# Keys and values of the first attention: seven part products (Strassen, in Winograd's form) for four of the five row blocks

## The reference

```python
xn = layernorm(x)
x = x + gnn(xn, W, edge_weight, src, dst) + mix(xn)      # L0
# mix:
ln1 = layer_norm(xn, gamma1, beta1)
q, k, v = ln1 @ wq, ln1 @ wk, ln1 @ wv                    # (625, 1024) each, 16 heads of 64
qp, kp = relu(q) + 0.001, relu(k) + 0.001
kvs = einsum('lhm,lhd->hmd', kp, v); ksum = sum(kp, 0)
att = einsum('lhm,hmd->lhd', qp, kvs) / einsum('lhm,hm->lh', qp, ksum)
add1 = att @ wo + xn
```

## Time and profile before

| | us |
|---|---|
| median of 3 runs | 1765.59 |
| lowest, highest | 1764.76, 1766.38 |
| span of the profiled execution | 1762.0 |
| TensorE busy | 1715.6 (97%) |
| VectorE busy | 743.4 (42%) |
| ScalarE busy | 396.1 (22%) |
| GpSimd busy | 653.0 (37%) |

### The profile page before, as it was taken

One profiled execution on the slowest core, in us unless ns is written; L12 is line 12 of the kernel. 1 busy time (PEld: TensorE's weight loads), 2 busy tenths in 40 slices (PEclk: granted clock), 3 DMA queues, 4 the chain that ended last, 5 costly groups with the idle time before them and its releaser, 6 DMA issues. The chain is left out here.

```text
span 1762.0 us, 21030 instructions
## 1 busy us (share of the span) xinstructions
PE 1715.6 (97%) x8016; PEld 1068.0 (61%) x8016; DVE 743.4 (42%) x1549; ACT 396.1 (22%) x740; POOL 653.0 (37%) x537
## 2 busy tenths in 40 slices
PE   9999999998999999999999999898999999999998
PEld 6466445544444677755477775555776676677633
DVE  5886011322732432154455553854333322222237
ACT  1100000001411000111177771841100222222232
POOL 0666884031000047767787862000210312222213
PEclk9999999998999999999999999999999999999999
DMA  9654116074170034333322223705262899999951
GB/s 352 200 168 123 2 1 167 1 214 120 73 297 5 0 96 127 98 96 101 92 49 57 53 48 79 195 11 195 60 198 87 351 415 415 400 415 411 412 150 59
DMA packets 103755, 281.71 MB, mean 160 GB/s; under 512 B 61745, under 2 KB 69155, under 8 KB 91282
## 3 DMA queue, kind: packets, MB, share of 16 engines
q1 hardware_dynamic: 28755, 218.54, 33.4%
q0 software_dynamic: 67872, 50.79, 12.8%
q10 hardware_dynamic: 7052, 11.35, 1.9%
HBM read 250.37 MB, written 29.80 MB: 159 GB/s over the span
## 5 line engine op out<-in xcount | busy, mean ns | idle before, releaser
L608 POOL DMA_INDIRECT table_d<-wring x85 | 173.9, 2046 | 106.3 <-issue 66.7
L380 PE MATMUL bank<-wring,region_a 128*125 128x512 f32 x480 | 207.6, 593 | 1.7 <-DVE region_a L754 0.7
L993 POOL DMA_INDIRECT wring<-xl_d,wring x85 | 111.2, 1308 | 255.2 <-DMA xr_d<-flat_b 229.3
L380 PEld LDWEIGHTS bank<-wring,region_a 128*125 128x125 f32 x480 | 89.7, 188 | 115.3 <-issue 113.9
L1006 POOL DMA_INDIRECT score_d<-wring x85 | 108.8, 1280 | 72.1 <-DMA score_d<-wring 42.7
L396 PE MATMUL bank<-flat_d,wring 128*128 128x312 f32 (+1 forms) x512 | 135.0, 426 | 0.0
L2403 PEld LDWEIGHTS bank<-picked_t,wring 128*128 128x128 f32 x1152 | 129.4, 192 | 7.7 <-issue 7.7
L2403 PE MATMUL bank<-picked_t,wring 128*128 128x128 f32 x1152 | 131.3, 276 | 0.0
L993 POOL DMA_INDIRECT wring<-xr_d,wring x85 | 110.4, 1299 | 25.9 <-issue 24.7
L396 PEld LDWEIGHTS bank<-flat_d,wring 128*128 128x128 f32 x512 | 96.8, 189 | 37.8
L2410 PE MATMUL bank<-wring,small_t 128*64 128x256 f32 x640 | 76.0, 393 | 2.8 <-PEq L2037 2.8
(11 more groups left out here) (441 smaller groups left out, 2671.6 us busy)
## 6 DMA issues: line engine op xcount, KB each, us to landing
wring<-in_experts SPq DMA_DIRECT2D x57, 2048.0 KB, 19.5
wring<-in_L_Ws SPq DMA_DIRECT2D x6, 2048.0 KB, 15.8
table_d<-eq_buf SPq DMA_DIRECT2D x2, 3072.0 KB, 26.9
score_d<-no_edge SPq DMA_DIRECT2D x2, 3072.0 KB, 32.1
wring<-table_d POOLq DMA_DIRECT2D x10, 610.4 KB, 7.1
wring<-score_d SPq DMA_DIRECT2D x5, 1093.8 KB
wring<-pid_d ACTq DMA_DIRECT2D x17, 312.5 KB, 3.8
wring<-in_edge_w ACTq DMA_DIRECT2D x17, 312.5 KB, 4.4
```

Of the source, the lines that this page charges most:

```text
L380: ins = pe.matmul(bank[0:R, :], act_t[:, k, tok(t)], w[:, k * HALF:(k + 1) * HALF], start=(k == 0), stop=(k == chunks - 1))
L608: pool.indirect_dma_start(out=tables_d[b % 2], out_offset=bass.IndirectOffsetOnAxis(ap=edge_at[:, b:b + 1], axis=0), in_=edge_sums[:, b, : ...
L993: pool.indirect_dma_start(out=to[:, g % 2, j, :], out_offset=None, in_=table, in_offset=bass.IndirectOffsetOnAxis(ap=index[:, b:b + 1], ax ...
```

## The change

For the first four row blocks, keys and values are now made by `pe_gemm_seven` in TensorE, `dve_gemm_seven` in VectorE and `act_gemm_seven` in ScalarE. The inputs are taken as 2 x 2 parts: A11, A12, A21, A22 (two row blocks of 250 rows, four pieces of the inner dimension each) and B11, B21, B12, B22 (four inner pieces, 512 columns each). Seven part products are made where the ordinary way has eight; every one is two row blocks by four pieces. Their inputs are sums: S1 to S4 of the activations, which lie in `pair_sums` (the freed `eq_buf` and a part of `rows_b`), and T1 to T4 of the weights, made in place in the weights' slots. The names in FILLS are TensorE's tiles in order, STEPS are VectorE's, COPIES are ScalarE's; each list is one semaphore. p1 and p2 share a bank, so do p7 and p4, and p5 and p3: the second is added to the first, after it has been read. The fifth row block is multiplied as before, and ScalarE copies it. The clip of the keys is no longer part of the reading of a bank: VectorE does it when all keys are in SBUF, in five passes, and TensorE waits for these ahead of line 551. The two slots of a matrix are freed near its end, the left one after p5_1, the right one after p3_1. So that the new semaphores fit, four of the second layer are replaced by older ones, with offsets.

```diff
--- before.py
+++ after.py
@@ -136,6 +136,35 @@
         return self.ring[:, slot, :]
 
 
+class Seven:
+    FILLS = ("last_left", "p1_0", "p1_1", "last_right", "p2_0", "p2_1", "p7_0", "p7_1", "p6_0", "p6_1",
+             "p4_0", "p4_1", "p5_0", "p5_1", "p3_0", "p3_1")
+    STEPS = ("s3", "s1_early", "s2", "t3", "t2", "t4", "s1", "u2_0", "u3_0", "u2_1", "u3_1", "t1", "s4",
+             "c21_0", "c21_1", "c22_0", "c22_1", "c12_0", "c12_1")
+    COPIES = ("c_left", "p1_0", "p1_1", "c_right", "c11_0", "c11_1")
+    def __init__(self, n, filled, stepped, copied):
+        self.filled, self.stepped, self.copied = filled, stepped, copied
+        self.fill_from, self.step_from, self.copy_from = (n * len(x) for x in (self.FILLS, self.STEPS, self.COPIES))
+    def copy(self, name):
+        return self.copy_from + self.COPIES.index(name) + 1
+    def fill(self, name):
+        return self.fill_from + self.FILLS.index(name) + 1
+    def step(self, name):
+        return self.step_from + self.STEPS.index(name) + 1
 def tok(t):
     return slice(t * R, (t + 1) * R)
 
@@ -413,6 +442,115 @@
                     ins.then_inc(d_filled, 1)
             wt.free(dring.filled, dring.made)
 
+        seven_sems = sem("seven_filled"), sem("seven_stepped"), sem("seven_copied")
+        X, W, Y, Z = (4, 5), (0, 1), (6, 7), (2, 3)
+        def pe_gemm_seven(pe, x, f, sums, before=None):
+            left = wt.take(pe)
+            def tile(bank, at, weights, k0, done, start=True):
+                for k in range(4):
+                    ins = pe.matmul(banks[bank][0:R, :], at(k), weights[:, (k0 + k) * HALF:(k0 + k + 1) * HALF],
+                                    start=start and k == 0, stop=k == 3, skip_group_check=not start)
+                if done:
+                    ins.then_inc(f.filled, 1)
+            def rows(k0, t):
+                return lambda k: x[:, k0 + k, tok(t)]
+            def summed(n, p):
+                return lambda k: sums[n][:, k, tok(p)]
+            def until(name):
+                pe.wait_ge(f.stepped, f.step(name))
+            def last(bank, weights):
+                for k in range(K):
+                    ins = pe.matmul(banks[bank][0:R, :], x[:, k, tok(T - 1)], weights[:, k * HALF:(k + 1) * HALF],
+                                    start=(k == 0), stop=(k == K - 1))
+                ins.then_inc(f.filled, 1)
+            last(Y[1], left)
+            if before:
+                pe.wait_ge(before.copied, before.copy("c11_1"))
+            for p in range(2):
+                tile(X[p], rows(0, p), left, 0, True)
+            right = wt.take(pe)
+            last(Y[0], right)
+            for p in range(2):
+                pe.wait_ge(f.copied, f.copy(f"p1_{p}"))
+                tile(X[p], rows(4, p), left, 4, True, start=False)
+            until("t3")
+            if before:
+                pe.wait_ge(before.stepped, before.step("c12_1"))
+            else:
+                dring.wait_empty(pe)
+            for p in range(2):
+                tile(Z[p], summed(0, p), right, 0, True)
+            until("t2")
+            pe.wait_ge(f.copied, f.copy("c_right"))
+            for p in range(2):
+                tile(Y[p], summed(1, p), left, 0, True)
+            until("t4")
+            for p in range(2):
+                until(f"u3_{p}")
+                tile(Z[p], rows(4, 2 + p), left, 4, True, start=False)
+            until("t1")
+            for p in range(2):
+                tile(W[p], summed(0, p), left, 0, True)
+            wt.free(f.filled, f.fill("p5_1"))
+            until("s4")
+            for p in range(2):
+                until(f"c22_{p}")
+                tile(W[p], summed(1, p), right, 4, True, start=False)
+            wt.free(f.filled, f.fill("p3_1"))
+        def act_gemm_seven(s, f, place, shaped):
+            for name, fill, bank, t, h in (
+                    ("c_left", "last_left", Y[1], T - 1, 0), ("p1_0", "p1_0", X[0], 0, 1), ("p1_1", "p1_1", X[1], 1, 1),
+                    ("c_right", "last_right", Y[0], T - 1, 1), ("c11_0", "p2_0", X[0], 0, 0),
+                    ("c11_1", "p2_1", X[1], 1, 0)):
+                s.wait_ge(f.filled, f.fill(fill))
+                s.activation(place(t, h), shaped(banks[bank][0:R, :]), ACT.Copy).then_inc(f.copied, 1)
+        def dve_gemm_seven(v, x, f, sums, slots, place, shaped, finish=None):
+            a11, a12 = x[:, 0:4, 0:2 * R], x[:, 4:8, 0:2 * R]
+            a21, a22 = x[:, 0:4, 2 * R:4 * R], x[:, 4:8, 2 * R:4 * R]
+            b11, b21, b12, b22 = (wring[:, slot, k0 * HALF:(k0 + 4) * HALF] for slot in slots for k0 in (0, 4))
+            def step(name, out, in0, in1, op=ALU.add, fill=None, after_step=None):
+                if fill:
+                    v.wait_ge(f.filled, f.fill(fill))
+                if after_step:
+                    v.wait_ge(f.stepped, f.step(after_step))
+                v.tensor_tensor(out, in0, in1, op).then_inc(f.stepped, 1)
+            def bank(n):
+                return shaped(banks[n][0:R, :])
+            step("s3", sums[0], a11, a21, ALU.subtract)
+            step("s1_early", sums[1], a21, a22)
+            step("s2", sums[1], sums[1], a11, ALU.subtract, after_step="s1_early")
+            step("t3", b12, b22, b12, ALU.subtract, fill="last_right")
+            step("t2", b11, b12, b11, after_step="t3")
+            step("t4", b21, b21, b11, ALU.subtract, fill="p2_1", after_step="t2")
+            step("s1", sums[0], a21, a22, fill="p7_1")
+            for p in range(2):
+                v.wait_ge(f.copied, f.copy(f"p1_{p}"))
+                step(f"u2_{p}", place(p, 1), bank(Y[p]), place(p, 1), fill=f"p6_{p}")
+                step(f"u3_{p}", place(2 + p, 1), bank(Z[p]), place(p, 1), after_step=f"u2_{p}")
+            step("t1", b11, b22, b11, ALU.subtract, fill="p6_1", after_step="t4")
+            step("s4", sums[1], a12, sums[1], ALU.subtract, after_step="s2")
+            for p in range(2):
+                step(f"c21_{p}", place(2 + p, 0), bank(Z[p]), place(p, 1), fill=f"p4_{p}", after_step=f"u2_{p}")
+            for p in range(2):
+                step(f"c22_{p}", place(2 + p, 1), bank(W[p]), place(2 + p, 1), fill=f"p5_{p}", after_step=f"u3_{p}")
+            for p in range(2):
+                step(f"c12_{p}", place(p, 1), bank(W[p]), place(p, 1), fill=f"p3_{p}", after_step=f"u2_{p}")
         def rows_tiles(v, halves=2):
 
             for h in range(halves):
@@ -471,7 +609,11 @@
         seen = above(CH_B)
         sel = above(CH_B)
         assert upper_at[0] <= 2 * 4096
-        kvs = rows_b.rearrange("p s k c -> p (s k c)")[:, 0:K * 2 * (DH + 1)].rearrange("p (k d) -> p k d", k=K)
+        KVS = K * 2 * (DH + 1)
+        kvs = rows_b.rearrange("p s k c -> p (s k c)")[:, 0:KVS].rearrange("p (k d) -> p k d", k=K)
+        pair_sums = [flat.rearrange("p (k n) -> p k n", k=4) for flat in (
+            eq_buf[:, 0:4 * 2 * R], rows_b.rearrange("p s k c -> p (s k c)")[:, KVS:KVS + 4 * 2 * R])]
+        keys_seven, values_seven = (Seven(n, *seven_sems) for n in range(2))
 
         lower = wring[:, 0:2, :].rearrange("p s c -> p (s c)")
         pairs = lower[0:R, 0:8 * N].rearrange("r (s k c) -> r s k c", s=2, k=2)
@@ -488,6 +630,7 @@
         mix_set, MIX_ONES, MIX_KVS = sem("mix_set"), 1, 2
         fills_set, FILL_ZEROS, FILL_NO_EDGE = sem("fills_set"), 1, 2
         spare_set = sem("spare_set")
+        keys_clipped = sem("keys_clipped")
 
         xn_t, ln1 = as_turned(flat_b), as_rows(flat_c)
         ints, floats = flat_d[:, 0:4 * P].bitcast(I32), flat_d[:, 4 * P:8 * P]
@@ -498,6 +641,16 @@
         PAIR = 2 * (DH + 1)
         GROUPS = ((0, 3), (3, 3), (6, 2))
         marks = {}
+        def key_rows(t, h):
+            return kp[:, t, h * HALF:(h + 1) * HALF]
+        def value_rows(t, h):
+            return vplus[:, t, h * HALF // DH:(h + 1) * HALF // DH, 0:DH]
+        def by_head(rows):
+            return rows.rearrange("r (h d) -> r h d", d=DH)
         TURN_AT, EARLY_CHUNKS = 3, 8
         TURN_NORM_AT = 4
         with nc.Block() as block:
@@ -540,10 +693,12 @@
                 sring.wait_empty(pe)
                 marks["s1_read"] = (dring.made, sring.made)
                 pe_gemm_cols(pe, ln1_t)
-                pe_gemm_rows(pe, ln1_t)
+                pe_gemm_seven(pe, ln1_t, keys_seven, pair_sums)
                 marks["keys_done"] = wt.freed[5]
-                pe_gemm_rows(pe, ln1_t)
-                pe_wait_evacuated(pe)
+                pe_gemm_seven(pe, ln1_t, values_seven, pair_sums, before=keys_seven)
+                pe.wait_ge(values_seven.stepped, values_seven.step("c12_1"))
+                pe.wait_ge(values_seven.copied, values_seven.copy("c11_1"))
+                pe.wait_ge(keys_clipped, T)
                 pe.wait_ge(mix_set, MIX_KVS)
                 for p in range(K):
                     bank = dring.produce(pe)
@@ -730,13 +885,12 @@
                         dve_chunk(v, EARLY_CHUNKS)
                     if n % 2:
```

(25 more changed lines are left out.)

## The result

| | before | changed |
|---|---|---|
| median | 1765.59 | 1755.56 |
| lowest, highest of 5 runs | 1764.76, 1771.06 | 1752.88, 1759.95 |
| span of the profiled execution | 1762.0 | 1753.3 |

The ratio is 0.9927, 95% interval 0.9902 to 0.9953, which is 13 us with an interval from 8 to 17 us; the medians stand 10.0 us apart. The forecast was 1752.0 us, range 1750.8 to 1757.6. So the measured time lies inside the range, 3.6 us above the forecast, and the first question of this part is whether those 3.6 us belong to the change.

The account below looks back on a forecast made before the run. TensorE alone was taken to bound keys and values. Span 1762.0 less 16 x 0.859 = 13.7, with added waits of 0.0 to 0.3, gave 1748.4; plus 3.6 from span to median, 1752.0 us, range 1750.8 to 1757.6.

Parts of the forecast that it names:

- The stage's bound and the term of the sum: Keys and values: TensorE alone bounds the stage; 16 products fewer at 0.859 us each take 13.7 us off.
- Prices on VectorE and ScalarE: Keys and values: row sums 1.19 us, weight sums 2.30, bank steps 0.692, ScalarE copies 0.59, clip passes 0.749 each.
- The handovers: VectorE's sums between TensorE's tiles: TensorE never waits; least left over is 1.8 us, at u3; sums cost nothing.
- GpSimd: Scattered additions beside VectorE's new work: slowed 9 us; line 605's kvs fill ends at 278, 7 us early, costing nothing.
- the reading of the stretch from 104 to 125 us: Scattered additions of line 608: one us of VectorE's SBUF work cost GpSimd 0.27 us by length, 0.65 with everything.
- The third rival: GpSimd locked out for all new SBUF work, 34.1 us; kvs fill ends at 302.9; net +3.9 us, 1769.5; 3%.
- Loads of wo: Halves issued at 277.6 and 284.5, landings 8.7 and 11.2 us, first product due at 311; 15 us to spare.
- So every later stage starts 13.7 us earlier: All stages after keys and values: loads and GpSimd's waits move along, so the whole 13.7 us is kept.
- The reading of the clock: Whole kernel: TensorE busy for 97% of the span, its granted clock in the top tenth in every slice.
- The base: Whole kernel before: median of the runs 1765.59 us, 3.6 us over the profiled execution's span of 1762.0.
- That 0.2% could be told from no change: Whole kernel: about 0.2%, 3.5 us, is what a measurement can tell from no change.

## Why the prediction was right, and where not

- **The stage's bound and the term of the sum**: right. 16 x 0.859 = 13.7 forecast, 13.74 measured from the keys' first product to the kvs step, and the same to 0.01 us in all seven other profiles of kernels with 16 products fewer and no added wait. No idle time of TensorE within 288 records.
- **Prices on VectorE and ScalarE**: right within 2 ns to 10 ns for sums, bank steps and copies. The clip took 0.812 us a pass instead of 0.749, but not because a pass is dearer: the shortest took 0.674, and single ones up to 1.147 while GpSimd's instructions ran beside them. That these held it up is likely and not shown by a run. It costs 0.3 us in a place with 12 us of slack.
- **The handovers**: right. No wait where 1.8 us were left over at the narrowest, and 0.87 us of loss once 2.50 us of work was put there.
- **GpSimd**: right in its sign, its size was overrated. I took 0.27 us lost for each us of VectorE's work, 9 us in all, with the fill of kvs ending at 278. The experiments gave 0.17 and 0.07, the comparison with the kernel before 0.13, and it ended at 270.1. The step that failed is the reading of the stretch from 104 to 125 us: the longer instructions there came with transfers of edge rows, and I put their whole excess down to VectorE. The third rival, with its 34 us, was an order of magnitude off against 4.4 us, and the reading behind it was too wide. The Trainium skill, "SBUF — State Buffer", section "SBUF: two separate sides", ties the lock for an operation with two SBUF inputs to GpSimd operations that read SBUF, and what it says of descriptors to modes that use both ports; I had carried both over to all sums and descriptors. The trace lies near the narrower rule: the median of the 47 instructions stays at 1.986 us, and a few beside the sums take up to 3.34.
- **Loads of wo**: right. Issued at 277.3 and 284.2, landed within 9 us, the first 24 us ahead of the product with wo.
- **"So every later stage starts 13.7 us earlier"**: right for four stages, then true only on average. This is the step where the 3.6 us went. In the profiled execution 3.3 us were lost in the feature loop, to a half-clock stretch that lasted 7 us longer, 1.9 to VectorE's longer wait for loads near the end, and the rest nearly cancels. That it is not the change's doing is shown by the kernel with products left out and no sums (1754.57), by the mean granted clock, which is 0.987 to 0.988 in every series of either kernel, and by the pair with the loop's gap filled, 13.9 us apart. For the 1.9 us the evidence is weaker: over all 14 profiles that stage took 69.9 to 72.8 us, in the five without the seven part products 70.3 to 71.8. Over the six comparisons of a kernel with and without the seven part products or the 16 products, means of one series, the gain was 10.6, 13.2, 12.3, 15.1, 13.9 and 11.9 us: 12.8 on average, around 13.7 (the second and third share the runs of the kernel before).
- **The reading of the clock**: the prediction says that the granted clock stands in the top tenth in every slice. Its own row has an 8 in the tenth slice, and the trace of the kernel before already held the 10 us at half clock in the feature loop. Read more closely, it would have warned of the scatter.
- **The base**: I started from 1765.59, a median of three runs within 1.6 us. Later runs of the same kernel ranged from 1761.6 to 1778.6, with medians of 1766 to 1770. The range that I gave, 6.8 us, took in the unknown costs of the change and nearly nothing of this scatter, which was the larger part. It held the time, in part by luck, for the reason that moved it was not in the range. That 0.2% could be told from no change was also too hopeful for five runs: the interval was a half of a per cent wide.

What stays open: what sets when the clock falls and how long it stays low. The two gaps at the loop's start are the same in all nine profiles, to 3 ns. In seven the clock fell 4.2 to 4.8 us after the loop's first product and stayed low for 10 us; in the changed kernel's two profiles it fell after 2.8 and 1.8 us (the last within the second gap) and stayed low for 14 and 17 us. The earlier fall goes with the longer stretch, and no run here varied that alone. These moments and lengths are worked out from the granted clock in rows as above.

## What to carry to other kernels

Where one engine is the bound and another has most of its time free in that stage, fewer products pay exactly their count, if each sum that they need is laid beside a tile that covers it: work out what is left over at each handover, and put the in-place sums and the second addition to a bank in that order. Before a saving of less than 1% is measured, look how far single runs of the unchanged kernel stand apart and what clock each was granted, and compare the stage itself in the two traces; the stage told 13.74 us from one profile, the whole needed dozens of runs to say 10 to 15. And look for idle gaps of some 2 us on TensorE just ahead of a dense stage: filling one with products that nobody reads was worth 4.4 us in the kernel before, a third of this whole change, for a few lines. See in the trace that they run inside the gap: those of the next stage did not.

## What the runs showed of the hardware

- A gap of 2.7 us of idle time in a stretch of 3.4 us (0.78 and 1.93 us, with 0.7 us of small products between) went in all nine profiles where it was left open with 10 to 17 us of TensorE at half clock; each us more at half clock cost about half a us (7 us more, 3.3 us). Filled with ten to eighteen products, it was followed by none in all five.
- Additions with two inputs in SBUF slowed the issue of GpSimd's scattered transfers by 0.07 to 0.17 us for each us of theirs; single instructions went from 1.99 to as much as 3.68 us, while the median stayed at 1.986. Beside the same transfers VectorE's clip took from 0.674 to 1.147 us a pass.
- TensorE adding to a bank that VectorE had read in between cost no time against a fresh one: 6.87 us from tile to tile in both cases.
